# Four copied half products in place of two scans that read their input from PSUM, in a two-layer state-space kernel

## The chip, the cores and the metric

One core of a Trainium2 chip runs one program that computes all 16 images. The metric is the time of one execution in device microseconds. Before the change the median of 3 runs is 21545.68 us (21533.71 to 21551.96).

## The reference, cut to what matters

Each image has 192 channels and 56x56 = 3136 positions. Layer 1 (an RWKV layer with a scan in both directions) is not touched. Layer 2 is a Mamba layer with 384 inner channels and 16 states for each, run once forward and once backward over the positions:

```
def step(h, inp):
    x_t, dt_t, B_t, C_t = inp
    dA = jnp.exp(dt_t[:, :, None] * A)
    h = h * dA + (dt_t * x_t)[:, :, None] * B_t[:, None, :]
    y = jnp.einsum('bdn,bn->bd', h, C_t)
```

For each channel and state four things are wanted at each position: the decay `exp(dt*A)`, the B product `(dt*x)*B`, the running `h`, and `h*C` summed over the states. `dt*x` is called `du` in the kernel.

## The kernel before, in words

The 3136 positions are 7 chunks of 448, taken forward (i = 0 to 6) and then backward (i = 7 to 13). A chunk has three tiles of 128 channels (e). A chunk's tile is called a **block** here (index r). A block's 16 states are eight **pairs** (q counts them over everything, p = 0 to 7 within a block). A pair is 128 rows by two runs of 448 columns with one column between them that carries the state from the previous chunk. There are 16 images x 14 chunks x 3 tiles = 672 blocks and 5376 pairs.

For each pair:
- ScalarE writes the two decays (L1370), one value between the runs (`reset`, L1380), and afterwards saves the last state (`carry`, L1388).
- One of three engines makes the B product: GpSimd (L1434) for p = 0, 2, 4; VectorE (L1206) for p = 1, 3, 5, from a copy of `du` that TensorE put into PSUM bank 4, `DUBANK` (job `dp`, L1013); TensorE (L1099) for p = 6, 7.
- VectorE runs the scan (L1222). It reads decays and products and writes `hh`.
- GpSimd multiplies by C (L1442), and TensorE adds over the states into bank 5, for two pairs at a time (L1123).

GpSimd's and VectorE's products go to a ring `bb` in SBUF of NB = 3 places, and the decays of those pairs to two double banks in PSUM (`DECAY`, banks 0 and 1 or 2 and 3). With TensorE's pairs it is the other way round: TensorE can write only PSUM, so its product goes into the pair's decay banks, and ScalarE writes the decays of these pairs into `bb`. The scan then takes its two inputs exchanged. TensorE's product is 16 matmuls (one for each of 2 states, 4 parts of 112 positions and 2 halves of the rows) of `duT`, the transposed `du` (jobs `dT`, TensorE, L1022, and `dS`, ScalarE, L1323), with `bz`, a block-diagonal arrangement of B that comes by DMA. A seventeenth matmul of one column (L1093) puts the carried state between the runs. When GpSimd's or VectorE's pair next uses the banks, ScalarE clears that column first (L1367).

Each engine works through one list in the order of steps g = q. VectorE at step g does scan(g), then a product for the pair g + 2, then the side jobs that are due. ScalarE at step g does the decays and the reset of pair g + 1, the carry of pair g - 1 (it waits for that scan), then its side jobs. TensorE at step g makes the product of pair g + 1 if it is its own (it waits for scan g - 1, since the banks must be free), then the sums for pairs g - 3 and g - 2 if g is odd, then its side jobs. GpSimd at step g does the output of pair g - 1, a product for pair g + 2, side jobs.

The side jobs prepare later blocks and finish earlier ones. `side_schedule` gives each a due time in steps, written out by hand: convolution (`cv`, TensorE L1054; `c1` to `c4` on ScalarE; `xc` on VectorE L1180), projections (`x` L1040, `xp` L1061 with `p1` on ScalarE L1304, `t` L1066 with `t1` L1310, `z` L1071, `o` L1078), the step size (`td`, L1186) and `du` (L1423). `ye` takes the finished sums out of bank 5: on ScalarE in the forward half (L1328, due early in step 1 of the next block), on VectorE in the backward half (L1193, due in step 2). The first matmul of the next block into bank 5 (L1115) waits for it. Every engine takes its list strictly in order, so a wait holds up all that follows on that engine.

## Time and profile before

| | |
|---|---|
| median of 3 runs | 21545.68 us |
| profiled execution | 21543.77 us |
| its span | 21542.0 us |
| TensorE busy, share of the span | 84% |
| VectorE busy | 77% |
| GpSimd busy | 74% |
| ScalarE busy | 63% |
| mean granted TensorE clock | 0.892 |

The 16 images take 1346 us each and are alike. A busy share is an average over both layers. The profile's TensorE matmuls are recorded as two records each (float32), and their ends are modelled.

### The profile page before, as it was taken

The page shows a single profiled execution, that of the slowest core. Times are in us where ns is not written, and L with a number is a line of the kernel's source. Part 1 is how long each engine was busy: PE and PEld are TensorE (multiplying, and loading weights), DVE is VectorE, ACT ScalarE, POOL GpSimd, SP SyncE. Part 2 cuts the span into 40 slices and gives each one's busy share as a digit, 9 for nine tenths or more (in the row PEclk, how much of TensorE's full clock was granted, in tenths as well). Part 3 has the DMA queues.
Part 4 walks back from the last instruction along what each step waited for, and adds up shares of the span by engine and source line. Part 5 has one row for each costly group of instructions (what it writes and reads, how often), then busy time and mean ns, then how long its engine had stood idle before and what let it go on. Part 6 is the DMA issues. An engine that isn't in the chain of part 4 may idle for free. (4 is left out here: it accounts for less than half of the span.)

```text
span 21542.0 us, 288881 instructions
## 1 busy us (share of the span) xinstructions
PE 18146.0 (84%) x93536; PEld 8343.5 (39%) x93536; DVE 16650.5 (77%) x12912; ACT 13602.1 (63%) x35141; POOL 15848.3 (74%) x10356
## 2 busy tenths in 40 slices
PE   7888888888888888888888888888888888888888
PEld 3433434344343443434434344343443434434344
DVE  7877878778787787877878778787787877878778
ACT  5656656566565665656656566565665656656566
POOL 5867868678686786867868678686786867768677
PEclk8988989889898898988989889898998989989899
DMA  2424424234242442424424244242442424324243
GB/s 73 110 59 100 110 63 109 63 99 108 63 109 63 100 106 63 109 64 100 105 63 109 64 101 104 63 109 64 103 102 63 110 65 105 98 63 111 64 108 96
DMA packets 1351547, 1906.07 MB, mean 88 GB/s; under 512 B 588266, under 2 KB 1094340, under 8 KB 1349892
## 3 DMA queue, kind: packets, MB, share of 16 engines
q1 hardware_dynamic: 1349892, 1886.24, 35.4%
q8 instruction: 766, 12.55, 0.3%
q14 instruction: 889, 7.28, 0.1%
HBM read 1160.53 MB, written 248.04 MB: 65 GB/s over the span
## 5 line engine op out<-in xcount | busy, mean ns | idle before, releaser
L1442 POOL TENSOR_TENSOR arena<-arena 128x896 f32<-128x896 f32 x5376 | 9442.9, 1765 | 3148.9 <-DVE arena L1222 2512.2
L1222 DVE TENSOR_TENSOR_SCAN arena<-ps,arena 128x897 f32<-128x897 f32 x4032 | 8263.6, 2066 | 626.5 <-POOL arena L1434 296.0
L1370 ACT ACTIVATE ps<-arena,A 128x448 f32<-128x448 f32 x8064 | 4782.6, 626 | 1056.3 <-DVE arena L1222 940.1
L1123 PE MATMUL ps<-arena,rep 128*64 128x448 f32 x21504 | 5181.4, 609 | 101.3 <-POOL arena L1442 101.3
L1222 DVE TENSOR_TENSOR_SCAN arena<-arena,ps 128x897 f32<-128x897 f32 x1344 | 2782.7, 2070 | 2610.0 <-PE ps L1099 856.6
L1434 POOL TENSOR_TENSOR arena<-arena 128x896 f32<-128x896 f32 x2016 | 3567.6, 1770 | 622.2 <-DMA arena<-arena 609.9
L1123 PEld LDWEIGHTS ps<-arena,rep 128*64 128x64 f32 x21504 | 1480.1, 151 | 3050.3 <-issue 2449.9
L1099 PE MATMUL ps<-arena 112*64 112x112 f32 x43008 | 2592.5, 278 | 0.0
L1099 PEld LDWEIGHTS ps<-arena 112*64 112x64 f32 x43008 | 2276.5, 147 | 20.2
L1054 PE MATMUL ps<-arena,diag 128*128 128x448 f32 x5248 | 2149.4, 553 | 111.8 <-ACT arena L1323 74.7
L1206 DVE TENSOR_TENSOR arena<-ps,arena 128x896 f32<-128x896 f32 x2016 | 2148.7, 1066 | 121.8 <-DMA arena<-bc_rows 121.8
L1370 ACT ACTIVATE arena<-arena,A 128x448 f32<-128x448 f32 x2688 | 1635.8, 658 | 0.0
L1115 PE MATMUL ps<-arena,skipd 128*128 128x448 f32 x1344 | 840.3, 713 | 901.3 <-DVE arena L1193 760.1
L1054 PEld LDWEIGHTS ps<-arena,diag 128*128 128x128 f32 x5248 | 968.3, 191 | 1223.4 <-issue 1039.7
L1066 PE MATMUL ps<-arena,wdt 13*128 13x448 f32 x1344 | 816.8, 717 | 508.0 <-DVE arena L1186 496.5
L1388 ACT ACTIVATE arena<-arena 128x2 f32<-128x2 f32 x5376 | 1034.8, 192 | 222.3 <-DVE arena L1222 221.7
L1323 ACT ACTIVATE arena<-ps 112x512 f32<-112x512 f32 x672 | 398.4, 593 | 1181.3 <-PE ps L1022 1181.2
L1423 POOL TENSOR_TENSOR arena<-arena 128x448 f32<-128x448 f32 x672 | 654.2, 978 | 512.8 <-DVE arena L1186 512.8
L1093 PE MATMUL ps<-arena,ident 128*128 128x1 f32 x2304 | 438.0, 259 | 663.7 <-DVE arena L1222 637.4
L1093 PEld LDWEIGHTS ps<-arena,ident 128*128 128x128 f32 x2304 | 408.7, 209 | 1421.3 <-DVE arena L1222 860.1
L868 POOL TENSOR_TENSOR arena<-arena 128x448 f32<-128x448 f32 x336 | 347.4, 1034 | 711.9 <-DVE arena L614 711.9
L1367 ACT ACTIVATE ps<-zero 128x1 f32<-128x1 f32 x1312 | 222.2, 169 | 980.8 <-DVE arena L1222 980.8
(184 smaller groups left out, 24756.2 us busy)
## 6 DMA issues: line engine op xcount, KB each, us to landing
arena<-bc_rows SPq DMA_DIRECT2D x3136, 224.0 KB, 4.9
arena<-arena SPq DMA_DIRECT2D x4160, 112.0 KB, 3.0
arena<-b_diagonals SPq DMA_DIRECT2D x224, 784.0 KB, 7.0
x_projected<-arena SPq DMA_DIRECT2D x112, 672.0 KB, 3.6
y_forward<-arena SPq DMA_DIRECT2D x112, 672.0 KB, 5.5
arena<-x_projected SPq DMA_DIRECT2D x112, 672.0 KB, 4.8
arena<-y_forward SPq DMA_DIRECT2D x112, 672.0 KB, 4.8
x<-in_x SPq DMA_DIRECT2D x119, 336.0 KB, 3.6
```

Source lines behind the costliest of these rows:

```text
L1054: m = e.matmul(o, diag[:, k, q, :], xh[i % 2][:, k, h:h + T], start=q == 0, stop=q == 3)
L1066: e.matmul(o, wdt[s][:, k * 128:(k + 1) * 128], res[0:R + 1, :], start=True, stop=True).then_inc(c_wt, 1)
L1093: e.matmul(ps[:, b, RS:RS + 1], ident[:, :], car[:, 2 * k + h, n:n + 1] if i % NC else zero[:, 0, 0:1], start=True, stop=True)
L1099: m = e.matmul(ps[64 * j:64 * j + 64, b + a, o:o + TB], duT[:, r % NDR, n, 64 * h:64 * h + 64], bz[:, n, (2 * j + a) * TB:(2 * j + a + 1) ...
L1115: e.matmul(y, skipd[:, s, k, :], xc[:, r % NXC, :], start=True, stop=False)
L1123: m = e.matmul(ps[64 * h:64 * h + 64, YBANK, 0:T], rep[:, 0:64], pr[:, (q - 1 + h) % NPR, a * T:a * T + T], start=False, stop=p == NP - 1 ...
L1206: e.tensor_tensor(two(bb[:, q % NB, :]), ps[:, DUBANK, 0:T].unsqueeze(1).to_broadcast([128, 2, T]), br[:, p - 1:p + 1, :], ALU.mult).then_ ...
L1222: e.tensor_tensor_scan(rev(hh[:, q % NH, 0:W2], s), rev(f, s), rev(b, s), car[:, 2 * k + p % 2, n:n + 1] if i % NC else 0.0, ALU.mult, ALU ...
L1370: e.activation(o[:, a, :], dt2[:, r % NR2, p % 2, :], ACT.Exp, scale=Am[s][:, 2 * k + p % 2, n:n + 1]).then_inc(c_ex, 1)
L1388: e.activation(car[:, 2 * k + p % 2, n:n + 2], h[:, 0:T1 + 1:T1] if s else h[:, T - 1:W2:T1], ACT.Copy).then_inc(c_ca, 1)
L1434: e.tensor_tensor(two(bb[:, q % NB, :]), du2[:, r % NR2, :].unsqueeze(1).to_broadcast([128, 2, T]), br[:, p:p + 2, :], ALU.mult).then_inc( ...
L1442: e.tensor_tensor(pr[:, q % NPR, :].rearrange("p (a b) -> p a b", a=2), two(hh[:, q % NH, :]), cr[:, p - p % 2:p - p % 2 + 2, :], ALU.mult ...
```

## The change

- TensorE's products no longer go to the decay banks. Each becomes two runs of 8 matmuls, one for each state (`sb`, four runs m = 0 to 3 in a block), written to columns 0 to 447 of `DUBANK`, one after another. After each run ScalarE copies the bank to the ring `bb` (`se`, 128x448). The runs are side jobs at steps 3.1, 4.1, 5.1 and 6.1 of their block, the copies at 3.6, 4.6, 5.6 and 6.3.
- A run waits for the copy of the run before, the first one for VectorE's last product of the block. `dp` waits for the block's last copy, and is due at the earliest one step later than before.
- The scan reads decays from PSUM and products from `bb` for every pair. The matmul of one column (L1093), ScalarE's clearing (L1367) and their waits go. `reset` puts the carried state in for all pairs.
- The ring `bb` has 4 places instead of 3.
- VectorE's products for p = 1, 3, 5 are made after scans 0, 1, 2 of the block (`LEAD`), where they were made after scan 7 of the block before, and scans 1 and 3.

```diff
-RS = 511
+LEAD = {1: 1, 3: 2, 5: 3}
-NB, NH, NPR = 3, 3, 4
+NB, NH, NPR = 4, 3, 4
...
-        pe.append((max(NP * (EJ * i + e) - 2, t + 4.5), "dp", i, e))
+        pe.append((max(NP * (EJ * i + e) - 1, t + 4.5), "dp", i, e))
...
+        for m in range(4):
+            o = NP * (EJ * i + e) + 3 + m
+            pe.append((o + 0.1, "sb", i, 4 * e + m))
+            act.append((o + (0.6 if m < 3 else 0.3), "se", i, 4 * e + m))
...
         else:
-            w.wait_ge(c_be, NE[q + 1])
+            w.wait_ge(c_ev, 2 * NE[q + 1])
...
                     w.wait_ge(c_bv, NV[NP * r])
+                    w.wait_ge(c_ev, 4 * r)
...
+                if name == "sb":
+                    k, m = divmod(k, 4)
+                    r = EJ * i + k
+                    h, a = divmod(m, 2)
+                    w.wait_ge(s_zl, 16 * (i + 1))
+                    freed(w, "dT", i, k)
+                    w.wait_ge(c_bv, NV[NP * (r + 1)])
+                    w.wait_ge(c_ev, 4 * r + m)
+                    for n in range(NTB):
+                        for j in range(2):
+                            m = e.matmul(ps[64 * j:64 * j + 64, DUBANK, TB * n:TB * n + TB],
+                                         duT[:, r % NDR, n, 64 * h:64 * h + 64],
+                                         bz[:, n, (2 * j + a) * TB:(2 * j + a + 1) * TB], start=True, stop=True)
+                    m.then_inc(c_be, 1)
...
-            if 0 <= g + 1 < Q and maker(g + 1) == PE:
-                product(g + 1)
...
-            if g + AHEAD < Q and maker(g + AHEAD) == DVE:
-                product(g + AHEAD)
+            for n in LEAD.values():
+                if 0 <= g + n < Q and maker(g + n) == DVE and LEAD[(g + n) % NP] == n:
+                    product(g + n)
...
+                if name == "se":
+                    k, m = divmod(k, 4)
+                    r = EJ * i + k
+                    q = NP * r + 6 + m // 2
+                    w.wait_ge(c_be, 4 * r + m + 1)
+                    w.wait_ge(c_sc, q - NB + 1)
+                    o = m % 2 * T1
+                    e.activation(bb[:, q % NB, o:o + T], ps[:, DUBANK, 0:T], ACT.Copy).then_inc(c_ev, 1)
...
-            if maker(q) == PE:
-                w.wait_ge(c_sc, q - NB + 1)
-                o = two(bb[:, q % NB, :])
-            else:
-                w.wait_ge(c_sc, q - 1)
-                o = two(decays(q))
-                if q > 1 and maker(q - 2) == PE:
-                    e.activation(ps[:, DECAY[q % 2], RS:RS + 1], zero[:, 0, 0:1], ACT.Copy).then_inc(c_rz, 1)
+            w.wait_ge(c_sc, q - 1)
```

## Rows read from the trace of the kernel before

**Rows 1.** The page's busy time, share and instructions by engine.

```profile
PE 18146.0 (84%) x93536; PEld 8343.5 (39%) x93536; DVE 16650.5 (77%) x12912; ACT 13602.1 (63%) x35141; POOL 15848.3 (74%) x10356
```

**Rows 2.** Busy time by stretch, layer 2, forward and backward half of one image.

```profile
core 0: us, PE busy (x) PEld busy (x) DVE busy (x) ACT busy (x) POOL busy (x), PEclk, DMA share, GB/s
4400.00:4850.00 450.00, 383.17 (x2185) 184.52 (x2185) 356.81 (x236) 298.54 (x804) 360.48 (x220) 0.90 0.40 101
4850.00:5395.00 545.00, 477.16 (x2704) 223.35 (x2702) 446.02 (x311) 362.51 (x978) 441.87 (x273) 0.92 0.42 105
```

**Rows 3.** Groups by line: count | busy, mean ns | idle before, releasers.

```profile
L1222 DVE TENSOR_TENSOR_SCAN arena<-ps,arena 128x897 f32<-128x897 f32 x4032 | 8263.6, 2066 | 626.5 <-POOL arena L1434 296.0 <-ACT arena L1388 208.8 <-ACT ps L1370 54.2
L1222 DVE TENSOR_TENSOR_SCAN arena<-arena,ps 128x897 f32<-128x897 f32 x1344 | 2782.7, 2070 | 2610.0 <-PE ps L1099 856.6 <-ACT arena L1388 697.2 <-ACT ps L1370 509.9
L1206 DVE TENSOR_TENSOR arena<-ps,arena 128x896 f32<-128x896 f32 x2016 | 2148.7, 1066 | 121.8 <-DMA arena<-bc_rows 121.8
L1093 PE MATMUL ps<-arena,ident 128*128 128x1 f32 x2304 | 438.0, 259 | 663.7 <-DVE arena L1222 637.4 <-issue 26.3
L1093 PE MATMUL ps<-zero,ident 128*128 128x1 f32 x384 | 70.5, 253 | 41.6 <-DVE arena L1222 40.9
L1099 PE MATMUL ps<-arena 112*64 112x112 f32 x43008 | 2592.5, 278 | 0.0
L1115 PE MATMUL ps<-arena,skipd 128*128 128x448 f32 x1344 | 840.3, 713 | 901.3 <-DVE arena L1193 760.1 <-ACT arena L1328 141.2
L1370 ACT ACTIVATE ps<-arena,A 128x448 f32<-128x448 f32 x8064 | 4782.6, 626 | 1056.3 <-DVE arena L1222 940.1 <-DMA arena<-arena 104.2
L1370 ACT ACTIVATE arena<-arena,A 128x448 f32<-128x448 f32 x2688 | 1635.8, 658 | 0.0
L1328 ACT ACTIVATE arena<-ps 128x448 f32<-128x448 f32 x336 | 178.6, 532 | 373.7 <-PE ps L1123 373.7
L1367 ACT ACTIVATE ps<-zero 128x1 f32<-128x1 f32 x1312 | 222.2, 169 | 980.8 <-DVE arena L1222 980.8
L1323 ACT ACTIVATE arena<-ps 112x512 f32<-112x512 f32 x672 | 398.4, 593 | 1181.3 <-PE ps L1022 1181.2
L1304 ACT ACTIVATE arena<-ps,ident 64x448 f32<-64x448 f32 x224 | 140.7, 628 | 999.3 <-PE ps L1061 999.3
```

**Rows 4.** Timeline, a backward block's last steps: start, us, engine, line [idle before <-releaser].

```profile
5026.77 3.27 PE L1054 MATMUL ps<-arena,diag 128*128 128x448 f32 x8
5029.88 0.28 PE L1093 MATMUL ps<-arena,ident 128*128 128x1 f32 x2
5030.09 1.54 PEld L1099 LDWEIGHTS ps<-arena 112*64 112x64 f32 x32
5030.09 1.75 PE L1099 MATMUL ps<-arena 112*64 112x112 f32 x32
5031.95 2.08 DVE L1222 TENSOR_TENSOR_SCAN arena<-arena,ps 128x897 f32<-128x897 f32 x1 [1.81 <-PE ps L1099]
```

**Rows 5.** Timeline, ScalarE over one step of the same block.

```profile
5024.64 1.20 ACT L1370 ACTIVATE ps<-arena,A 128x448 f32<-128x448 f32 x2
5025.77 0.19 ACT L1380 ACTIVATE arena<-arena 128x1 f32<-128x1 f32 x1
5025.86 0.19 ACT L1388 ACTIVATE arena<-arena 128x2 f32<-128x2 f32 x1
5025.95 0.62 ACT L1335 ACTIVATE arena<-ps,bxz 128x448 f32<-128x448 f32 x1
```

**Rows 6.** Timeline, TensorE after two long waits, backward and forward.

```profile
5075.19 1.46 PE L1115 MATMUL ps<-arena,skipd 128*128 128x448 f32 x2 [4.86 <-DVE arena L1193]
5078.36 3.25 PE L1123 MATMUL ps<-arena,rep 128*64 128x448 f32 x8
5083.82 1.67 PE L1123 MATMUL ps<-arena,rep 128*64 128x448 f32 x8
...
4513.03 0.59 PE L1093 MATMUL ps<-arena,ident 128*128 128x1 f32 x2 [4.78 <-DVE arena L1222]
4513.55 3.25 PE L1099 MATMUL ps<-arena 112*64 112x112 f32 x32
```

**Rows 7.** Busy time by stretch around those waits; the granted clock is the seventh number.

```profile
5075.00:5082.00 7.00, 6.81 (x14) 2.02 (x14) 6.70 (x5) 4.04 (x12) 4.92 (x5) 0.54 0.86 208
4513.00:4517.00 4.00, 3.97 (x36) 3.78 (x38) 2.62 (x3) 1.68 (x7) 3.74 (x3) 0.50 0.00 0
```

**Rows 8.** Timeline, TensorE before a product of a forward block.

```profile
4484.11 1.77 PE L1040 MATMUL ps<-arena,wx 96*128 96x448 f32 x4
4485.72 3.17 PE L1054 MATMUL ps<-arena,diag 128*128 128x448 f32 x8
4488.93 1.75 PE L1099 MATMUL ps<-arena 112*64 112x112 f32 x32
```

More of the change, by code:

```diff
@@ L167, in side_schedule @@
     release = {(name, i, e): read.get((last.get(name), i, e)) for _, name, i, e in plans[0]}
-    for k, (t, name, i, e) in enumerate(a for a in plans[0] if a[1] != "dp"):
+    for k, (t, name, i, e) in enumerate(a for a in plans[0] if a[1] not in ("dp", "sb")):
         banks = WBANK if t >= -10 else [*WBANK, 0, 1, 2, 3]
@@ L1082, in side @@
                     busy(e, *behind.get((name, k), (0, 0)))
-        def product(q):
-            r, i, k, p, s = pair(q)
-            b, h = DECAY[q % 2], p % 2
-            w.wait_ge(s_zl, 16 * (i + 1))
-            freed(w, "dT", i, k)
-            w.wait_ge(c_sc, q - 1)
-            n = p - h + 1 - s
-            if i % NC:
-                w.wait_ge(c_ca, q - PER + 1)
-            e.matmul(ps[:, b, RS:RS + 1], ident[:, :], car[:, 2 * k + h, n:n + 1] if i % NC else zero[:, 0, 0:1],
-                     start=True, stop=True)
-            for a in range(2):
-                for n in range(NTB):
-                    for j in range(2):
-                        o = (RS - T) * (1 - a) + TB * n
-                        m = e.matmul(ps[64 * j:64 * j + 64, b + a, o:o + TB],
-                                     duT[:, r % NDR, n, 64 * h:64 * h + 64],
-                                     bz[:, n, (2 * j + a) * TB:(2 * j + a + 1) * TB], start=True, stop=True)
-            m.then_inc(c_be, 1)
         side(-10)
         for g in range(-2, Q + LAG):
-            if 0 <= g + 1 < Q and maker(g + 1) == PE:
-                product(g + 1)
             q = g - LAG
@@ L1137, in layer1_vector @@
         for b in DECAY:
-            e.memset(ps[:, b, RS:RS + 1], 0.0)
+            e.memset(ps[:, b, T:T1], 0.0)
         steps = Steps(plan_dve)
@@ L1216, in scan @@
             n = p - p % 2 + s
-            f, b = decays(q)[:, 0:W2], bb[:, q % NB, 0:W2]
-            if maker(q) == PE:
-                f, b = b, f
-            if maker(q - 2) == PE and maker(q) != PE and q > 1:
-                w.wait_ge(c_rz, NE[q - 1])
-            e.tensor_tensor_scan(rev(hh[:, q % NH, 0:W2], s), rev(f, s), rev(b, s),
+            e.tensor_tensor_scan(rev(hh[:, q % NH, 0:W2], s), rev(decays(q)[:, 0:W2], s), rev(bb[:, q % NB, 0:W2], s),
                                  car[:, 2 * k + p % 2, n:n + 1] if i % NC else 0.0, ALU.mult, ALU.add).then_inc(c_sc, 1)
@@ L1359, in decay @@
                     w.wait_ge(c_wf[b], first.get(b, 0))
[L1360 to L1367 removed]
+            w.wait_ge(c_sc, q - 1)
             for a in range(2):
                 n = p - p % 2 + a
[L1370 removed]
+                e.activation(two(decays(q))[:, a, :], dt2[:, r % NR2, p % 2, :], ACT.Exp,
                              scale=Am[s][:, 2 * k + p % 2, n:n + 1]).then_inc(c_ex, 1)
@@ L1376, in reset @@
             w.wait_ge(c_sc, q - NB + 1)
-            given = i % NC and maker(q) != PE
-            if given:
+            if i % NC:
                 w.wait_ge(c_ca, q - PER + 1)
-            e.activation(bb[:, q % NB, T:T1], car[:, 2 * k + p % 2, n:n + 1] if given else zero[:, 0, 0:1],
+            e.activation(bb[:, q % NB, T:T1], car[:, 2 * k + p % 2, n:n + 1] if i % NC else zero[:, 0, 0:1],
                          ACT.Copy).then_inc(c_rs, 1)
```

14 lines of the change are left out of this document (6 added, 8 removed).

## The prediction

> **What bounds the kernel now.** I read the page's busy times first. TensorE is busiest with 84%, VectorE 77%, GpSimd 74%, ScalarE 63% [rows 1]. No engine is full, so the waits decide. Only layer 2 changes, so next come the stretches inside layer 2: TensorE 383 of 450 us forward and 477 of 545 backward (85 and 88%), VectorE 79 and 82%, GpSimd 80 and 81%, ScalarE 66 and 67% [rows 2]. Then the groups by line, for the idle time before each. VectorE's scans of GpSimd's and its own products waited 626.5 us in 4032 scans. The scans that take TensorE's product waited 2610.0 us in 1344, which is 1.94 us each and 12% of the span [rows 3]. Only 856.6 us of that ended with TensorE's product. 697.2 and 509.9 us ended with ScalarE's carry and decays, and ScalarE in turn waits for TensorE: 1181.3 us before the copy of the transposed `du`, 999.3 us before the projection's copy [rows 3]. TensorE waits for VectorE: 663.7 + 41.6 us before the one-column matmul and 760.1 us before L1115, for `ye` [rows 3]. So the bound is a circle of three in-order queues, and TensorE, with the least idle time, is the one that is late. A row of it: a convolution of 3.27 us stands ahead of the product, the product starts 2 us late, and the scan waits 1.81 us [rows 4].
>
> **The change, part by part.** All sums are over the 672 blocks, against the profiled execution's 21543.8 us. The median shown is 1.9 us above that, so it needs no scaling.
>
> (a) The one-column matmul and its wait for scan g - 1 go. Busy 438.0 + 70.5 us, idle before it 663.7 + 41.6 us, together 1213.8 us of TensorE's queue, 1.81 us a block [rows 3]. Since TensorE is the late queue, I count this whole as the gain. If it were not late, the wait would only turn up at its next instruction. The ends are 0 and 1214.
>
> (b) Two products become four runs. The matmuls stay the same. A product takes 1.75 us (2592.5 / 1344 = 1.93 us on average [rows 3]) while its weight loads take 1.54 [rows 4], so each start costs about 0.21 us of filling. Two more starts a block are 672 x 0.42 = 282 us. The ends are 0 (the next work follows in the pipe) and 282. I take 282, because a run's end is now what ScalarE waits for.
>
> (c) A run waits for the copy of the run before. No row of before has this copy, but `ye` on ScalarE is the same shape from PSUM to SBUF: 532 ns [rows 3]. Runs 0 and 2 are followed by TensorE's next step with no sums in between for runs 1 and 3, so two waits a block can show: 672 x 2 x 0.53 = 712 us. In the backward list a side job stands in between in three of six places (the convolution due at 3.5, `xp` at 13.1, `dT` and `z` at 21.1 and 21.6), and hides the copy. I take half, 356 us. The ends are 0 and 712.
>
> (d) VectorE's products move to after scans 0, 1 and 2. In the backward half `ye` is due in step 2 and now has the product for p = 5 ahead of it, 1066 ns [rows 3]. L1115 waits for `ye`, and behind L1115 in TensorE's queue are the sums and run 0. 336 backward blocks x 1.066 = 358 us. If also the product moved into step 0 counts, it is 716. If TensorE is late anyway, it is 0. I take 358, since TensorE does wait here today. In the forward half ScalarE's `ye` is in step 1, and I put this at nothing.
>
> (e) ScalarE gets four copies a block and loses the clearing (222.2 us in all) and 32 ns on each of 2688 decays that now go to PSUM (658 against 626 ns) [rows 3]: 2688 x 0.532 - 222 - 86 = 1122 us more work. A step's fixed work takes 1.31 us, from the start of the decays to the start of the side job [rows 5]. With a copy it is 1.84, under a scan's 2.07. ScalarE is idle a third of layer 2, so I take 0. That cover is gone wherever the copy comes late (the second rival). The upper end is 1122.
>
> (f) The fourth place costs nothing and brings little. GpSimd's product for g + 2 stands behind the output of g - 1, which waits for the same scan that frees a place of three. It lets the copies for p = 6 start one scan earlier. DMA issues are the same in number and bytes. `bl`, which waits for products, comes free no later. `dp` is due one step later and waits for the last copy; it has until the end of the next block's scan 0, some 4 us for its 1 us. I take 0, up to 100 if it is late in a block of three.
>
> Sum: 1214 - 282 - 356 - 358 = 218 us less, 0.32 us a block. 21543.8 - 218 + 1.9 = 21328, say **21,330 us**, 1.0% faster. What is late next is the same circle: the convolution still stands ahead of run 1 or run 3, and a scan still waits for it.
>
> **Rivals.** *Much faster: the circle opens.* The products leave the banks that the scans alternate in, and no longer need to be made within one scan's time. If the waits that ended with TensorE's product go and nothing takes their place, it is 21545 - 857 = 20,690 us. If half of the other 1753 us goes too, it is 19,810. For it speaks that the run 0 could be made early. Against it: the due times put all four runs and copies into steps 3 to 6, right before the scans that need them, and and the idle time before all scans, 626.5 + 2610.0 us [rows 3], is only 4.8 us a block to begin with.
>
> *Slower: late copies hold ScalarE, and ScalarE holds every scan.* Before, TensorE's lateness reached ScalarE only at the side jobs. Now ScalarE stops at four places a block, in steps 3 to 6, behind TensorE's queue, and the decays of two pairs on stand behind each copy. ScalarE can be some 0.7 us late (2.07 - 1.31) before a scan waits [rows 5]. In the first forward block of a chunk `x` and the convolution, 1.77 + 3.17 us [rows 8], stand between run 0 and run 1. With the run's own 0.9 us that is 5.8 us in a step that gives 2.07 and a slack of 0.7: a scan would wait 3.0 us, against the 1.94 us that a scan with TensorE's product waits today on average, so 112 x 1.1 = 120 us. In the backward half `ye` is later, TensorE sits idle at L1115 for longer, and afterwards it is slow: after an idle of 4.86 us the granted clock is 0.54, near the lower of the two levels, and sums take 3.25 us instead of 1.67; after 4.78 us of idle a product takes 3.25 instead of 1.75 at a clock of 0.50 [rows 6, 7]. The sums lose 1.6 us, and L1115 takes 1.46 us against 840.3 / 672 = 1.25 on average [rows 3], together 1.8 us. In the backward chunk that I read, one block of three has such a wait today. In the other two it would come new: 224 x 1.8 = 400 us, all of it ahead of run 0. 21,545 - 218 + 120 + 400 = 21,850 us. It decides from 0.32 us a block of scans held up by late copies.
>
> The Trainium skill, "TensorE: Matmul & The Clock Gate", section on HAM oscillation, says that a loop which waits between bursts of matmuls falls back to the low clock and starts each burst slow. The trace agrees in the rows of that rival. By the rule without the trace the new waits of the backward half would each start the next burst at half speed, which is this rival's time and not the forecast's.
>
> *No change.* The 1.81 us that (a) frees is met by as much waiting for copies: (b), (c) and (d) at their upper ends are 282 + 712 + 716 = 1710, at their lower ones 0, and 1214 lies inside. That is 21,545 us.
>
> **How the numbers follow.** I give the forecast 0.33, the much faster case 0.24, no change 0.10, slower 0.33. A change of 0.2% (43 us) is about what a measurement of this kernel can tell from none. So faster by more has 0.57, within it 0.10, slower 0.33. The forecast's own range is 21,000 to 21,500. The whole range reaches into both rivals, 20,500 to 22,000 us: below it lies the part of the much faster case in which ScalarE's waits go as well (0.08), above it a slower case in which copies hold up more than two blocks in three (0.10).
>
> **What would show it.** (a) TensorE's busy share in the stretches of layer 2 rises above 85 and 88%, and none of its product's matmuls waits for a scan. (b, c) Each run is 16 records and starts within 0.2 us of its copy's end where no side job stands between. (d) L1115's idle time behind the backward `ye` grows from 760 by about 360 us. (e) The new copies take 0.53 us. If they show large idle times before them, above 1.5 us each, and the scans for p = 5 and 6 wait for ScalarE's decays, the slower rival is right. If the waits before the scans for p = 6 and 7 fall from 2610 to below 1700 us with none new elsewhere, the much faster one is. The granted clock falls below 0.89 in the slower case and rises in the others. I am wrong if scans at p = 4 and 5, which wait little today, take over the waiting.

## The result and the profile after

The changed kernel takes 22606.12 us, the median of 4 runs (22592.56 to 22633.41). The kernel before takes 21539.69 us beside it (21522.74 to 21551.96, 4 runs). The ratio is 1.0497 with an interval of 1.0479 to 1.0515, so it is 1066 us slower. I had forecast 21,330 us, within 20,500 to 22,000. Both are missed. Of the rivals the one on the slower side came nearest (21,850 us).

The page's busy times of the changed kernel, against [rows 1]:

```profile
PE 18112.9 (80%) x90848; PEld 8004.3 (35%) x90848; DVE 16684.3 (74%) x12912; ACT 14585.3 (65%) x36517; POOL 15864.4 (70%) x10356
```

Its stretches of one image, forward and backward half, against [rows 2], and seven microseconds after a long wait of TensorE, against [rows 7]:

```profile
core 0: us, PE busy (x) PEld busy (x) DVE busy (x) ACT busy (x) POOL busy (x), PEclk, DMA share, GB/s
4600.00:5050.00 450.00, 372.56 (x2114) 169.89 (x2111) 353.85 (x233) 321.86 (x832) 350.93 (x214) 0.91 0.40 100
5095.00:5655.00 560.00, 446.40 (x2430) 202.40 (x2426) 412.23 (x287) 358.88 (x933) 404.29 (x249) 0.88 0.36 91
5210.00:5217.00 7.00, 6.36 (x45) 3.33 (x46) 0.88 (x1) 2.42 (x7) 3.60 (x3) 0.66 0.93 224
```

TensorE's share is 83% forward and 80% backward. It had been 85 and 88%, and I had said it would rise. The busy times of the engines are within 35 us of those before, apart from ScalarE's, which is 983 us longer. So time went into waiting, and the backward half shows most of it. From the first to the last of one image's 21 `ye` that half takes 568.4 us in place of 508.9. The forward half takes 523.2 in place of 518.8. Times 16 images these are 952 and 70 us, together 1022 of the 1049 us between the two profiled spans.

The groups by line of the changed kernel. The scan is L1215, VectorE's product L1204, `dp` L1018, `xc` L1178, `td` L1184, `ye` L1191 (backward) and L1330 (forward). The first matmuls of a block into bank 5, which wait for `ye`, are L1113; they are called the **skip products** here. The sums are L1121, the runs L1031, the copies L1320, decays and carry L1365 and L1382, and VectorE's part of the output is L1196:

```profile
L1215 DVE TENSOR_TENSOR_SCAN arena<-ps,arena 128x897 f32<-128x897 f32 x5376 | 10998.2, 2067 | 3294.6 <-ACT arena L1382 1881.0 <-ACT arena L1320 826.5 <-POOL arena L1428 463.1
L1204 DVE TENSOR_TENSOR arena<-ps,arena 128x896 f32<-128x896 f32 x2016 | 2161.0, 1072 | 528.3 <-PE ps L1018 528.3
L1178 DVE SCALAR_TENSOR_TENSOR arena<-ps,vece,arena 128x448 f32<-128x448 f32 x672 | 451.9, 672 | 502.8 <-ACT arena L1290 502.8
L1184 DVE SCALAR_TENSOR_TENSOR arena<-ps,arena 128x448 f32<-128x448 f32 x672 | 405.5, 614 | 423.3 <-ACT arena L1312 423.3
L1196 DVE SCALAR_TENSOR_TENSOR x<-ps,bout,x 96x448 f32<-96x448 f32 x224 | 151.0, 674 | 239.7 <-PE ps L1098 239.7
L1320 ACT ACTIVATE arena<-ps 128x448 f32<-128x448 f32 x2688 | 1446.7, 538 | 3091.0 <-PE ps L1031 3089.4
L1031 PE MATMUL ps<-arena 112*64 112x112 f32 x43008 | 2798.7, 271 | 574.0 <-ACT arena L1320 552.9 <-DVE arena L1204 14.6
L1113 PE MATMUL ps<-arena,skipd 128*128 128x448 f32 x1344 | 932.0, 785 | 1234.9 <-DVE arena L1191 1127.7 <-ACT arena L1330 105.8
L1121 PE MATMUL ps<-arena,rep 128*64 128x448 f32 x21504 | 5289.8, 618 | 392.2 <-POOL arena L1436 378.2
```

Four rows of the kernel before, for comparison: `xc`, `td` and the output job of VectorE (L1178, L1184, L1196 after the change) and TensorE's sums (L1121 after).

```profile
L1180 DVE SCALAR_TENSOR_TENSOR arena<-ps,vece,arena 128x448 f32<-128x448 f32 x672 | 448.2, 667 | 300.3 <-ACT arena L1296 300.3
L1186 DVE SCALAR_TENSOR_TENSOR arena<-ps,arena 128x448 f32<-128x448 f32 x672 | 405.1, 613 | 190.9 <-ACT arena L1318 190.9
L1198 DVE SCALAR_TENSOR_TENSOR x<-ps,bout,x 96x448 f32<-96x448 f32 x224 | 151.4, 676 | 59.9 <-PE ps L1078 59.9
L1123 PE MATMUL ps<-arena,rep 128*64 128x448 f32 x21504 | 5181.4, 609 | 101.3 <-POOL arena L1442 101.3
```

Read this as two accounts of idle time. **VectorE** is idle 1015 us more (22590.7 - 16684.3 against 21542.0 - 16650.5). The scans have only 58 of it, 3294.6 in place of 626.5 + 2610.0 [rows 3]. The other waits grew: the products for `dp` by 406, `xc` by 203, `td` by 232, L1196 by 180. But the scans wait for something else. TensorE's product ended 856.6 us of their waits before, and ScalarE's carry some 906 in the two groups together [rows 3]. Now the carry ends 1881.0 us and the copies 826.5. **TensorE** is idle 1082 us more, though the 705 us before the one-column matmul are gone. The waits that came are 574 before the runs, 334 before the skip products (1234.9 against 901.3), and 291 before the sums. Its busy time fell by 33 us only, though 508 us of one-column matmuls went: the runs took 206 more, the sums 108, the skip products 92.

The timeline of one backward block of the changed kernel (start, us, engine, line, and in brackets the idle time before and its releaser), against [rows 6]:

```profile
5206.29 0.61 DVE L1191 TENSOR_TENSOR arena<-arena,ps 128x448 f32<-128x448 f32 x1
5206.96 1.86 PE L1113 MATMUL ps<-arena,skipd 128*128 128x448 f32 x2 [5.55 <-DVE arena L1191]
5208.75 1.86 PE L1086 MATMUL ps<-arena,wdt 13*128 13x448 f32 x2
5210.54 3.26 PE L1121 MATMUL ps<-arena,rep 128*64 128x448 f32 x8
5210.64 0.55 ACT L1304 ACTIVATE arena<-ps 128x448 f32<-128x448 f32 x1 [4.33 <-PE ps L1086]
5213.58 1.50 PE L1031 MATMUL ps<-arena 112*64 112x112 f32 x16
5215.13 0.54 ACT L1320 ACTIVATE arena<-ps 128x448 f32<-128x448 f32 x1 [3.94 <-PE ps L1031]
5215.57 1.19 ACT L1365 ACTIVATE ps<-arena,A 128x448 f32<-128x448 f32 x2
5215.73 0.99 PE L1031 MATMUL ps<-arena 112*64 112x112 f32 x16 [0.65 <-ACT arena L1320]
5216.54 1.68 PE L1121 MATMUL ps<-arena,rep 128*64 128x448 f32 x8
5217.06 2.08 DVE L1215 TENSOR_TENSOR_SCAN arena<-ps,arena 128x897 f32<-128x897 f32 x1 [6.19 <-ACT arena L1382]
...
5237.82 1.86 PE L1113 MATMUL ps<-arena,skipd 128*128 128x448 f32 x2 [4.67 <-DVE arena L1191]
5242.35 1.72 PE L1121 MATMUL ps<-arena,rep 128*64 128x448 f32 x8
5244.89 0.55 ACT L1320 ACTIVATE arena<-ps 128x448 f32<-128x448 f32 x1 [7.18 <-PE ps L1031]
5246.82 2.08 DVE L1215 TENSOR_TENSOR_SCAN arena<-ps,arena 128x897 f32<-128x897 f32 x1 [4.49 <-ACT arena L1382]
```

TensorE stands idle for 5.55 us until `ye` is done. Then it is slow: the sums take 3.26 us and not 1.68. So run 0 ends more than 8 us after `ye` began. ScalarE has first waited 4.33 us for the projection `t` (L1086), which stands behind the skip products as well. Then it has reached copy 0 and waits 3.94 us for run 0. The decays of p = 5 stand behind this copy, though they need nothing from it, and the scan of p = 5 starts 6.19 us late.

The slow sums of this block are not new. The kernel before had 4.86 us of idle time and sums of 3.25 us in its block of the same kind [rows 6]. Its scan of p = 5 there waited 0.30 us:

```profile
5080.40 2.08 DVE L1222 TENSOR_TENSOR_SCAN arena<-ps,arena 128x897 f32<-128x897 f32 x1 [0.30 <-ACT arena L1388]
```

What is new here is that ScalarE waits for run 0, so that TensorE's lateness reaches the decays.

The three blocks of a backward chunk differ. From one `ye` to the next the changed kernel takes 30.9, 33.2 and 24.7 us (starts 5206.29, 5237.16, 5270.37, 5295.05), where the kernel before takes 25.9, 26.3 and 26.2 us in blocks of the same kinds. In the second block the skip products wait 4.67 us and are slow (1.86 us for the pair), but the sums run at full speed (1.72 us). Copy 0 waits 7.18 us, and the scan of p = 5 waits 4.49. In the third the skip products wait for nothing, and the block is 1.5 us shorter than before. So two blocks of three lose, and the slow clock came new in one of them.

### The profile page after: what moved, and what is told of

The parts are those of the page before. It is cut to its first block and busy times, and to the rows that moved or that the text cites. A ratio compares the mean times of both kernels' runs of the same rounds, so it can differ in the third digit from the quotient of the medians.

```text
span 22590.7 us, 281969 instructions
## 1 busy us (share of the span) xinstructions
PE 18112.9 (80%) x90848; PEld 8004.3 (35%) x90848; DVE 16684.3 (74%) x12912; ACT 14585.3 (65%) x36517; POOL 15864.4 (70%) x10356
## 5 line engine op out<-in xcount | busy, mean ns | idle before, releaser
L1215 DVE TENSOR_TENSOR_SCAN arena<-ps,arena 128x897 f32<-128x897 f32 x5376 | 10998.2, 2067 | 3294.6 <-ACT arena L1382 1881.0
L1365 ACT ACTIVATE ps<-arena,A 128x448 f32<-128x448 f32 x10752 | 6399.8, 631 | 1671.1 <-DVE arena L1215 1536.7
L1121 PE MATMUL ps<-arena,rep 128*64 128x448 f32 x21504 | 5289.8, 618 | 392.2 <-POOL arena L1436 378.2
L1320 ACT ACTIVATE arena<-ps 128x448 f32<-128x448 f32 x2688 | 1446.7, 538 | 3091.0 <-PE ps L1031 3089.4
L1031 PE MATMUL ps<-arena 112*64 112x112 f32 x43008 | 2798.7, 271 | 574.0 <-ACT arena L1320 552.9
L1031 PEld LDWEIGHTS ps<-arena 112*64 112x64 f32 x43008 | 2372.3, 144 | 1850.5 <-issue 924.8
L1121 PEld LDWEIGHTS ps<-arena,rep 128*64 128x64 f32 x21504 | 1463.8, 150 | 3369.1 <-issue 2240.4
L1204 DVE TENSOR_TENSOR arena<-ps,arena 128x896 f32<-128x896 f32 x2016 | 2161.0, 1072 | 528.3 <-PE ps L1018 528.3
L1113 PE MATMUL ps<-arena,skipd 128*128 128x448 f32 x1344 | 932.0, 785 | 1234.9 <-DVE arena L1191 1127.7
L1086 PE MATMUL ps<-arena,wdt 13*128 13x448 f32 x1344 | 775.2, 684 | 560.6 <-DVE arena L1184 473.8
L1382 ACT ACTIVATE arena<-arena 128x2 f32<-128x2 f32 x5376 | 1040.5, 194 | 33.9 <-DVE arena L1215 33.9
L1374 ACT ACTIVATE arena<-arena 128x1 f32<-128x1 f32 x4608 | 883.3, 192 | 0.0
L1113 PEld LDWEIGHTS ps<-arena,skipd 128*128 128x128 f32 x1344 | 275.1, 244 | 1675.1 <-DVE arena L1191 1297.7
L1098 PE MATMUL ps<-arena,wout 128*96 128x448 f32 x1344 | 690.9, 665 | 167.5 <-ACT arena L1354 167.5
L1178 DVE SCALAR_TENSOR_TENSOR arena<-ps,vece,arena 128x448 f32<-128x448 f32 x672 | 451.9, 672 | 502.8 <-ACT arena L1290 502.8
L1091 PE MATMUL ps<-arena,wz 96*128 96x448 f32 x1344 | 708.0, 659 | 57.3 <-ACT arena L1325 37.4
```

The source lines that it names most:

```text
L1031: m = e.matmul(ps[64 * j:64 * j + 64, DUBANK, TB * n:TB * n + TB], duT[:, r % NDR, n, 64 * h:64 * h + 64], bz[:, n, (2 * j + a) * TB:(2 * ...
L1113: e.matmul(y, skipd[:, s, k, :], xc[:, r % NXC, :], start=True, stop=False)
L1121: m = e.matmul(ps[64 * h:64 * h + 64, YBANK, 0:T], rep[:, 0:64], pr[:, (q - 1 + h) % NPR, a * T:a * T + T], start=False, stop=p == NP - 1 ...
L1204: e.tensor_tensor(two(bb[:, q % NB, :]), ps[:, DUBANK, 0:T].unsqueeze(1).to_broadcast([128, 2, T]), br[:, p - 1:p + 1, :], ALU.mult).then_ ...
L1215: e.tensor_tensor_scan(rev(hh[:, q % NH, 0:W2], s), rev(decays(q)[:, 0:W2], s), rev(bb[:, q % NB, 0:W2], s), car[:, 2 * k + p % 2, n:n + 1 ...
L1320: e.activation(bb[:, q % NB, o:o + T], ps[:, DUBANK, 0:T], ACT.Copy).then_inc(c_ev, 1)
```

## The experiments

Times are medians. The kernel before took 21,540 to 21,555 us beside each.

### Where `ye` stands

*ye in step 1* (the changed kernel):

```
-                dve.append((t + 1.5, "ye", i, e))
+                dve.append((t + 0.5, "ye", i, e))
```

> The changed kernel with one number different: the backward half's ye on VectorE is due in step 1 of the next block (t + 0.5) and not in step 2, so that it stands ahead of scan 2 and of the product for p = 5. Theory A (the loss comes from ye behind VectorE's three early products: TensorE idles at L1113, is slow afterwards, run 0 is late, ScalarE waits for it): the backward half gets most of its 57 us an image back, 22,606 goes to 21,700 to 21,900, L1113's idle time falls from 1235 us to below 600. Theory B (the copies themselves are due too close behind their runs, whatever ye does): less than 300 us come back, 22,300 or more.

Measured: 21635.36 us, ratio 1.0037 [1.0021, 1.0053]. One due time gives back 971 of the 1066 us.

```profile
L1215 DVE TENSOR_TENSOR_SCAN arena<-ps,arena 128x897 f32<-128x897 f32 x5376 | 10982.3, 2067 | 2368.0 <-ACT arena L1320 947.6 <-ACT arena L1382 840.0 <-POOL arena L1428 457.1
L1113 PE MATMUL ps<-arena,skipd 128*128 128x448 f32 x1344 | 749.1, 642 | 397.4 <-DVE arena L1191 286.4 <-ACT arena L1330 109.6
```

The scans lose 927 us of idle time; what ended with the carry falls by 1041, what ended with copies grows by 121. The skip products and sums behind one `ye`:

```profile
5114.10 1.02 PE L1113 MATMUL ps<-arena,skipd 128*128 128x448 f32 x2 [1.69 <-DVE arena L1191]
5116.69 1.72 PE L1121 MATMUL ps<-arena,rep 128*64 128x448 f32 x8
5118.24 0.94 PE L1031 MATMUL ps<-arena 112*64 112x112 f32 x16
5119.23 0.55 ACT L1320 ACTIVATE arena<-ps 128x448 f32<-128x448 f32 x1 [1.73 <-PE ps L1031]
```

This is a block of the second kind. The skip products wait 1.69 us in place of 4.67 and take 1.02 us in place of 1.86. Run 0 ends 5.7 us after `ye` began, and copy 0 waits 1.73 us in place of 7.18. Two blocks of the first kind, where `t` stands between skip products and sums:

```profile
5087.29 1.02 PE L1113 MATMUL ps<-arena,skipd 128*128 128x448 f32 x2 [1.57 <-DVE arena L1191]
5089.34 3.21 PE L1121 MATMUL ps<-arena,rep 128*64 128x448 f32 x8
...
5167.95 1.02 PE L1113 MATMUL ps<-arena,skipd 128*128 128x448 f32 x2 [0.74 <-DVE arena L1191]
5169.84 1.72 PE L1121 MATMUL ps<-arena,rep 128*64 128x448 f32 x8
```

In this image two early chunks of the half still have slow sums there, behind idle times of 1.81 and 1.57 us; the chunks after them have 0.74 us and sums at full speed. Three blocks take 78 to 80 us, as before the change. TensorE's granted clock rises from 0.886 to 0.912, and its busy time falls by 435 us for the same instructions (17678.0 in place of 18112.9).

*ye in step 2, ahead of the product for p = 5.* This is the 1.07 us that my term (d) charged:

```
-                if 0 <= g + n < Q and maker(g + n) == DVE and LEAD[(g + n) % NP] == n:
+                if n < 3 and 0 <= g + n < Q and maker(g + n) == DVE and LEAD[(g + n) % NP] == n:
...
+            if g + 3 < Q and (g + 3) % NP == 5:
+                product(g + 3)
```

> The changed kernel with ye still in step 2 (after scan 2, with that step's other side jobs), but VectorE's product for p = 5 put behind the side jobs instead of ahead of them. It takes away only the 1.07 us of that product from ye; ye in step 1 took away the product and scan 2, 3.1 us, and gave 971 us. If the prediction's term (d) is the whole of it: about 336 x 1.07 = 360 us come back, 22,250. If it is a threshold (TensorE's idle time before L1113 just long enough for the low clock): 600 us or more. If ye's place behind scan 2 is what counts: less than 150.

Measured: 22606.9 us, ratio 1.0496 [1.0475, 1.0517], as the changed kernel. Two groups, and TensorE's timeline behind one `ye`:

```profile
L1113 PE MATMUL ps<-arena,skipd 128*128 128x448 f32 x1344 | 861.1, 730 | 894.2 <-DVE arena L1191 779.5 <-ACT arena L1332 113.3
L1121 PE MATMUL ps<-arena,rep 128*64 128x448 f32 x21504 | 5519.8, 641 | 393.5 <-POOL arena L1438 378.8
```

```profile
5221.11 1.86 PE L1113 MATMUL ps<-arena,skipd 128*128 128x448 f32 x2 [3.01 <-DVE arena L1191]
5224.69 3.11 PE L1121 MATMUL ps<-arena,rep 128*64 128x448 f32 x8
```

The wait at the skip products shrank by 341 us, which is just 336 x 1.01. But 3.01 us of idle are followed by nearly the same slow sums (3.11 us) as 5.55 us were. TensorE's busy time is 380 us longer (18492.5) at a clock of 0.869, and its idle time is 360 us shorter (22610.0 - 18492.5 = 4117.5 against 4477.8). What the shorter waits gave went into slower matmuls. So (d) had the size of the idle time right, and taking this idle time away by itself gives nothing back.

*ye in step 1 in the kernel before:*

```
-                dve.append((t + 1.5, "ye", i, e))
+                dve.append((t + 0.5, "ye", i, e))
```

> The kernel before with ye in step 1 alone. VectorE's product for p = 5 is not in step 2 there (it is in step 3), so ye moves only past one scan, and may wait for TensorE's sums. Theory A: a small gain or none, 21,350 to 21,600, since L1115's idle time of 901 us is partly ye's. If it gains as much as the changed kernel did (971 us), the change was not what made ye's place expensive, and theory A is wrong.

Measured: 21873.39 us, ratio 1.0153 [1.0124, 1.0182]. There the same edit costs 332 us. The wait at the skip products halves as well, and `ye` now waits for the sums (339.3 us; 116.7 before it was moved):

```profile
L1115 PE MATMUL ps<-arena,skipd 128*128 128x448 f32 x1344 | 785.1, 670 | 424.7 <-DVE arena L1193 282.9 <-ACT arena L1328 141.8
L1193 DVE TENSOR_TENSOR arena<-arena,ps 128x448 f32<-128x448 f32 x336 | 207.2, 617 | 339.3 <-PE ps L1123 339.3
```

### The places of VectorE's products

*The kernel before with the change's places for the products, and nothing else:*

```
+LEAD = {1: 1, 3: 2, 5: 3}
...
-            if g + AHEAD < Q and maker(g + AHEAD) == DVE:
-                product(g + AHEAD)
+            for n in LEAD.values():
+                if 0 <= g + n < Q and maker(g + n) == DVE and LEAD[(g + n) % NP] == n:
+                    product(g + n)
```

> The kernel before with VectorE's products made after scans 0, 1 and 2 (the LEAD edit alone; no runs, no copies, three places). Theory A in its plain form says that ye comes a product later here too and TensorE idles at L1115 longer: 21,540 goes up by 300 to 500 us. Theory C (ye is only harmful together with copies that ScalarE takes in order): within 150 us of 21,540, L1115's idle time up by 300 us all the same. Theory B says no change.

Measured: 22081.77 us, ratio 1.0254 [1.0224, 1.0284], 530 us slower. So a loss half as large comes without any run or copy.

```profile
L1223 DVE TENSOR_TENSOR_SCAN arena<-arena,ps 128x897 f32<-128x897 f32 x1344 | 2784.8, 2072 | 2883.7 <-PE ps L1100 1337.4 <-ACT arena L1390 776.7 <-ACT arena L1382 306.2
L1116 PE MATMUL ps<-arena,skipd 128*128 128x448 f32 x1344 | 887.2, 750 | 1287.3 <-DVE arena L1194 1152.6 <-ACT arena L1330 134.7
```

*Only p = 5 moved* (`{1: 2, 3: 2, 5: 3}`):

> The kernel before with VectorE's product for p = 5 alone moved, from after scan 3 to after scan 2. All three moves together cost 530 us, and ye in step 1 did not give them back. Theory D: VectorE's products fill time in which TensorE and ScalarE catch up; taken out of steps 3 to 7 they leave five scans in a row, and the wait before pairs 6 and 7 grows by what they covered. The product for p = 5 leaves step 3, just before TensorE's pairs: I expect 150 to 350 us. In the backward half it also puts ye 1.07 us later.

Measured: 21684.82 us, 1.0057 [1.0034, 1.008], 130 us.

*Only p = 1 moved* (`{1: 1, 3: 2, 5: 2}`):

> The kernel before with the product for p = 1 alone moved, from after scan 7 of the block before to after scan 0. Theory D: it leaves step 7 and enters step 0; TensorE's pair 7 has just been scanned, the next pairs are GpSimd's and VectorE's, and little waits there: 50 to 250 us. The two moves add up to about 530 if each only takes its own cover away; if they sum to much less, it is the row of five scans that costs, and only both together make it.

Measured: 21809.95 us, 1.0119 [1.0089, 1.0148], 255 us. This product stands ahead of `ye` in VectorE's list before and after the move, and the move still costs twice what that of p = 5 does. I had put it at nothing. The two make 385 of the 530 us.

*Both, the products' places and `ye` in step 1, in the kernel before:*

> The kernel before with both VectorE edits: products after scans 0, 1, 2, and ye in step 1. No runs, no copies. Theory A: the 530 us that the early products cost alone come back, 21,450 to 21,650; what then lies between this and the changed kernel with ye in step 1 (21,635) is the price of runs and copies. The rival (the early products hurt by their place before the scans, not by ye): 21,900 or more.

Measured: 22032.07 us, 1.0227 [1.0197, 1.0256]. The wait at the skip products falls from 1287.3 to 449.9 us, and the time by 50. In this kernel, too, that wait is not what the products' places cost.

These kernels make a table on which the change's parts can be read:

| us | ye in step 2 | ye in step 1 |
|---|---|---|
| before | 21,545 | 21,873 |
| + products' places | 22,082 | 22,032 |
| + runs, copies, fourth place (the change) | 22,606 | 21,635 |

The runs and copies cost 524 us in the one column and gain 397 in the other. They have no price of their own.

### The copies

Two kernels shrink the copies or the runs; each leaves out part of the computation, as its expectation says.

*Thin runs*, from the changed kernel:

```
-                    for n in range(NTB):
+                    for n in range(1):
```

> The changed kernel with each run of TensorE cut from 8 matmuls to 2 (three quarters of the B products of pairs 6 and 7 are left out), all waits and copies kept. If TensorE's own work is what is late (the convolution and the sums ahead of a run, and the run): about 0.6 us less for each of four runs a block, 1600 us of TensorE's queue, and the time falls by 600 us or more. Theory A: the waits stay where they are, since they are for VectorE's ye and for the copy, and the time falls by less than 400 us.

Measured: 22070.61 us (one run).

*Short copies:*

```
-                    e.activation(bb[:, q % NB, o:o + T], ps[:, DUBANK, 0:T], ACT.Copy).then_inc(c_ev, 1)
+                    e.activation(bb[:, q % NB, o:o + 16], ps[:, DUBANK, 0:16], ACT.Copy).then_inc(c_ev, 1)
```

> The changed kernel with each of ScalarE's copies cut from 448 columns to 16 (the rest of the B products of pairs 6 and 7 stays out of the ring), all waits kept. Takes away some 0.36 us of each copy, 970 us of ScalarE's work. If ScalarE's added work were the cost, 600 us or more come back. Theories A and B both say that ScalarE is held by waiting, not by work: less than 350 us come back, and the 3091 us of idle time before the copies stay above 2500.

Measured: 22235.31 us (one run). The group of its copies:

```profile
L1320 ACT ACTIVATE arena<-ps 128x16 f32<-128x16 f32 x2688 | 479.4, 178 | 3481.4 <-PE ps L1031 3477.8
```

967 us of ScalarE's work bring 371 us, and the wait before the copies grows by 390. With a quarter of the matmuls in the runs, 536 us come back, between the two outcomes that were expected. TensorE's mean granted clock falls to 0.854 there, and the sums take 5553.4 us in place of 5289.8, so a part of what the thin runs save is lost again. Nor is it a price of the change, since the same matmuls were there before it. With either, the kernel is still 2.4 to 3.2% slower than before. So neither length by itself makes up the 1066 us; what is left lies in the waits and in the moved products.

*Copies on VectorE, ye in step 1*, to see what ScalarE's place in the chain costs:

```
-            act.append((o + (0.6 if m < 3 else 0.3), "se", i, 4 * e + m))
+            dve.append((o + 0.9, "se", i, 4 * e + m))
```

> The changed kernel with ye in step 1 and the four copies on VectorE, at the end of the steps in which they were on ScalarE. ScalarE then has no wait for a run and no work of 1450 us; VectorE gets 4 x 0.55 us a block, 1480 us, on its own scans' queue. If what costs is ScalarE's decays held by late runs: the decays are never late, but VectorE itself stops for each run; I expect 21,900 to 22,600, slower than 21,635, because VectorE has less to spare. A time below 21,600 would say that the copies' place on ScalarE was the fault.

Measured: 21582.03 us, 1.0026 [1.0014, 1.0037].

```profile
L1224 DVE TENSOR_TENSOR_SCAN arena<-ps,arena 128x897 f32<-128x897 f32 x5376 | 11074.8, 2068 | 541.9 <-POOL arena L1429 389.8 <-issue 26.2 <-ACT ps L1366 16.5
L1155 DVE COPY arena<-ps 128x448 f32<-128x448 f32 x2688 | 1638.8, 610 | 1243.5 <-PE ps L1031 1242.7
```

With no copy in ScalarE's list the scans hardly wait for ScalarE: 541.9 us of idle time in place of 2368.0 with `ye` in step 1, which is 1826 less. This fits waits at the carry that came through the copies. It does not prove it, because VectorE now stops ahead of its own copies and gives ScalarE time. VectorE pays 1638.8 us of copying and 1243.5 of waiting for the runs, together 2882. I had expected 21,900 us or more. The median lies 53 us under that of the version with ScalarE's copies, but the ranges overlap (21550.76 to 21641.79 against 21613.14 to 21639.58). By my own mark (below 21,600) the copies' place on ScalarE was at fault, but 53 us with overlapping ranges are too little to rest that on. Other waits of VectorE shrink as well, `dp` from 531.3 to 183.2 us.

### Other places for runs, copies and side jobs

*Runs ahead of the sums* (`o - 0.05` in place of `o + 0.1`, with ye in step 1):

> The changed kernel with ye in step 1 and each run due just before its step (2.95, 3.95, 4.95, 5.95), so that TensorE makes runs 0 and 2 before the sums of steps 3 and 5. If copies wait for runs because 1.5 us of sums stand ahead of runs 0 and 2: the idle time before the copies falls from 2140 us to below 1500 and the time below 21,400. If TensorE is then only made to wait for the copy before or for VectorE's product instead: within 100 us of 21,635, or slower.

Measured: 21965.03 us, 1.0196 [1.0166, 1.0225]. The scans wait 2894.2 us in all, against 2368.0. The rival of the expectation came true: TensorE waits 509.0 us for VectorE's product before the runs, where it waited 23.2, and 1191.1 before the runs in all, where it was 613.5. The wait of `ye` for the sums did not grow (313.0 us against 325.0).

*Backward convolutions and input projection moved out of steps 3 to 6* (with ye in step 1):

```
-            for e, v in enumerate((1.3, 6.0, 10.7)):
+            for e, v in enumerate((1.3, 8.7, 11.0)):
...
-            project(i, t + 15.6, (1.9, 2.3, 5.2), 1.5)
+            project(i, t + 16.7, (1.0, 1.4, 4.3), 0.9)
```

> The changed kernel with ye in step 1, and in the backward half the two TensorE jobs that stood between a block's runs put behind its last run: the convolution due at 3.5 goes to 6.2 (the next from 8.2 to 8.5), the projection xp with what hangs on it from 13.1 to 14.2. If the copies wait because a job of 2.2 to 3.3 us stands between two runs: the 2140 us of idle time before the copies fall below 1600 in the backward half's share, and the time below 21,450. If the wait only moves to what these jobs feed (c1, p1, the step size, GpSimd's du): within 100 us of 21,635.

Measured: 22825.45 us, 1.059 [1.0559, 1.062].

*The same with the copies on VectorE:*

> The same with the copies on VectorE. Measured with the old places: 21,582 against 21,635 with the copies on ScalarE. If the places of the jobs matter for whoever waits for the runs, this gains as much as the previous kernel does, to 21,400 or below, and beats the kernel before; if VectorE is now full (84% busy), less than 50 us.

Measured: 22926.52 us, 1.0637 [1.0606, 1.0667], 101 us more than with the copies on ScalarE.

*Convolutions alone moved* (`(2.0, 8.7, 11.0)`, so that the first has another place too):

> The changed kernel with ye in step 1 and only the backward convolutions moved: from 22.8, 3.5 and 8.2 to 23.5, 6.2 and 8.5; xp and what follows stay. The version with xp moved too was 1190 us slower than without. If that came from xp (its chain to du, GpSimd's product and the DMA is late): this one is within 200 us of 21,635, and below it if a job between runs 0 and 1 costs. If it came from the convolutions: 22,500 or more.

Measured: 22117.99 us, 1.0269 [1.0249, 1.029]. All three miss. In the first VectorE waits 737.0 us for `dp`, against 531.3 without the move, the scans 2853.4 against 2368.0, and `ye` 684.1 against 325.0, nearly all of it for the sums. With the convolutions alone `ye` waits 574.2 us. What within these moves costs so much was not taken apart further.

*The p = 1 product back after scan 7* (`{1: 2, 3: 2, 5: 3}`, with ye in step 1):

> The changed kernel with ye in step 1 and the product for p = 1 back after scan 7 of the block before, as before the change (p = 3 and p = 5 stay after scans 1 and 2). In the kernel before, moving p = 1 cost 255 us and p = 5 130 us. Theory D (the product covers a wait of the late steps) expects 100 to 255 us less than 21,635, a tie with the kernel before or a little better. The rival: the product for p = 1 needs du in PSUM bank 4, which TensorE can write only after the block's last copy, so VectorE now waits for it before scan 0 instead of after it: 21,650 to 22,000.

Measured: 22877.13 us, 1.062 [1.0603, 1.0638].

```profile
L1204 DVE TENSOR_TENSOR arena<-ps,arena 128x896 f32<-128x896 f32 x2016 | 2163.3, 1073 | 1777.4 <-PE ps L1018 1654.3 <-DMA arena<-bc_rows 122.0
```

`dp` can't come before the last copy has left the bank, and a product that asks for it a step earlier waits 1654.3 us for it instead of 531.3. So the change needs its late p = 1, and pays for it.

*The same with copies on VectorE:*

> The same with the copies on VectorE (21,582 with the product for p = 1 after scan 0). As above: theory D 21,330 to 21,500, the rival 21,650 or more. Here the last copy is VectorE's own, at the end of step 6, so that bank 4 comes free a little later.

Measured: 22430.58 us, 1.041 [1.0393, 1.0428]. Both are slower than even their rival range from 21,650 to 22,000 us.

*Runs and copies spread, ye in step 2.* This takes copy 0 from its place half a step behind run 0:

```
-            pe.append((o + 0.1, "sb", i, 4 * e + m))
-            act.append((o + (0.6 if m < 3 else 0.3), "se", i, 4 * e + m))
+            pe.append((o + (0.1, 0.6, 0.4, 0.1)[m], "sb", i, 4 * e + m))
+            act.append((o + (1.2, 1.1, 0.9, 0.3)[m], "se", i, 4 * e + m))
```

> The changed kernel with the backward ye where the change has it (step 2), but the runs spread (steps 3.1, 4.6, 5.4, 6.1) and each copy one step or so behind its run (steps 4.2, 5.1, 5.9, 6.3), in place of runs at 3, 4, 5, 6 and copies half a step behind them. If the price is the tight chain ye, skip and sums, run 0, copy 0, decays of p=5 on ScalarE, then copy 0's idle time goes and much of the 1066 us comes back with ye still in step 2: 21,700 to 22,100 us, clock above 0.89. If the price is ye's place itself (TensorE's idle time at the skip products, then half clock, whoever waits for the copies), nothing comes back: 22,500 to 22,700 us. If the later copies reach the output step too late, 22,800 us or more.

Measured: 22925.91 us, 1.0641 [1.0611, 1.067].

*The same with ye in step 1:*

> The same spread runs and copies with the backward ye in step 1. If copy 0 and copy 1 still hold ScalarE in that kernel (947 us of the scans' idle time lay behind the copies in the changed kernel with ye in step 1), this gives 21,350 to 21,500 us and beats the kernel before. If the places of the sums and side jobs are what counts, the moved runs cost as in the other moved versions: 21,900 to 22,300 us. No effect: 21,600 to 21,700 us.

Measured: 22397.05 us, 1.0391 [1.037, 1.0413]. The scans of the two:

```profile
L1215 DVE TENSOR_TENSOR_SCAN arena<-ps,arena 128x897 f32<-128x897 f32 x5376 | 10981.1, 2066 | 3860.7 <-ACT arena L1320 3015.4 <-POOL arena L1428 431.2 <-ACT arena L1382 197.2
```

```profile
L1215 DVE TENSOR_TENSOR_SCAN arena<-ps,arena 128x897 f32<-128x897 f32 x5376 | 10972.4, 2066 | 3327.2 <-ACT arena L1320 2599.3 <-POOL arena L1428 431.3 <-POOL arena L1436 196.5
```

The decays came free of the copies: the carry ends 197.2 us of the first kernel's waits, in place of 1881.0. This is the strongest sign that the waits at the carry came through the copies. But the scans of p = 6 and 7 then wait for the copies themselves, 3015.4 us. Both hopes failed. Steps 3 to 6 are tight from both sides: an early copy holds the decays, a late one holds its own scan. `ye` in step 1 gives 529 us here, where it gave 971 with the change's own places.

No version that I tried is faster than the kernel before.

## Why the prediction was wrong, by its own steps

**(a), the step that failed.** I counted the one-column matmul and its wait, 1214 us, as gain, since TensorE was the late queue. The instruction and the wait did go. But the time freed did not become time saved: in the changed kernel TensorE waits at other places, for engines that had not become earlier. The new waits before runs and sums, 574 + 291 us, already outweigh the 705 us of old ones. I had written that the wait would turn up at the next instruction if TensorE were not late, and then gave that case no weight in the sum. With (a) at its lower end of 0 and the other terms as taken the sum gives 21,546 + 996 = 22,542 us, close to the 22,606 measured. This is luck: (d) has 358 of the 996, and the run that takes its 1.07 us away gains nothing.

**(b)** was about right: the runs have 206 us more busy time than the products (282 forecast), and a run takes 0.94 to 0.99 us where half a product took 0.875.

**(c)** was too small as a wait: 553 us of TensorE's waits before the runs end with a copy, against 356, within my ends of 0 and 712.

**(d)** named a wait that grew as forecast, by 368 us behind the backward `ye` (760.1 to 1127.7) against 358. But an idle time is not a cost. Moving `ye` ahead of the product took 341 us of the wait before the skip products away and gave nothing back. Moving it a whole step earlier gave 971 us. I had also put the product that moved into step 0 at nothing in the value that I took. In the kernel before it alone costs 255 us, and p = 5 130.

**(e)** I took as covered by ScalarE's idle third. The copies' own length is worth some 371 us, as the short copies show. Their waits are 3091.0 us, 1.15 each, with the decays queued behind. This is not idle time on top: ScalarE is idle 8005 us in all (22590.7 - 14585.3), where it was 7940 (21542.0 - 13602.1). The 980.8 us before the clearing went, and 1181.3 us before the copy of the transposed `du` became 84.9. The waits moved to a place ahead of the decays.

**(f)** I gave `dp` 4 us to spare and at most 100 us. VectorE's products wait 528.3 us for it, where 121.8 us had ended with a DMA [rows 3].

**The slower rival** had the mechanism: copies hold ScalarE, ScalarE holds the scans through decays and carry, TensorE idles at the skip products and is then slow. The spread copies show that the carry's waits came through the copies (1881.0 us became 197.2), and the timeline shows the chain whole in one block of three. One of its marks was off: the copies' idle time was 1.15 us on average and not above 1.5. The others held: in the blocks shown the scan of p = 5 waits for ScalarE, 6.19 and 4.49 us, and the mean granted clock fell from 0.892 to 0.886. That p = 5 takes over the waiting was also my sign of being wrong. Its size, 305 us, was under a third of the 1066: I priced the slow clock behind each `ye` (400) and late copies of the forward half (120), and took the forecast's gain of 218 off. That gain is (a)'s, and it is not in the measured time. I had the slow clock come new in two blocks of three; in the steady chunks it came new in one, and that one's sums are not slow. The trace shows 952 us in the backward half and 70 in the forward one. What I left out were `dp` (406 us at VectorE), its jobs `xc`, `td` and L1196 (615 us, behind ScalarE and TensorE) and the products' new places.

The Trainium skill says, in "TensorE: Matmul & The Clock Gate", section on HAM oscillation, that a loop with waits between its bursts starts each burst slow. The runs agree in part. After 5.55 us and after 3.01 us of idle the sums take 3.26 and 3.11 us, after 0.74 us of idle with `ye` in step 1 they take 1.72. But with `ye` in step 1 they also took 3.21 us after 1.57 us of idle, and in the changed kernel 1.72 us after 4.67, where the skip products ahead of them were the slow ones (1.86 us). The length of the one wait ahead of a burst did not settle its speed.

**What stays open.** The table of six kernels shows that `ye`, the products' places and the runs don't add up, and no run names one link by which `ye` becomes 971 us. Copy 0's early place stands in the chain of the timeline, but spreading runs and copies made things worse. No run was made in which TensorE's clock alone differs, so how much of the 971 us the 435 us of faster matmuls make is not shown either.

## What to carry to other kernels

When three in-order queues wait for each other, idle time removed from one is no gain until a run shows that nothing else holds it. Ask of each wait which instruction stands behind it that does not need it; here the decays of p = 5 stood behind a copy that they did not need. And try the schedule edits of a change (places, due times) by themselves before the change that needs them: here the products' places cost 530 us alone, and one due time was worth 971.

## What the runs showed of the hardware that I had not expected

- A shorter wait of TensorE can come with a lower granted clock and be worth nothing. With `ye` 1 us earlier TensorE's idle time fell by 360 us and its busy time rose by 380 for the same 90848 instructions, the mean clock going from 0.886 to 0.869.
- The other way round, the version with `ye` in step 1 ran the same instructions in 435 us less at a mean clock of 0.912. That is as much as 45% of the 977 us between the two spans; that the clock alone brings it is not shown.
- An ACTIVATE copy of 128x448 from PSUM to SBUF took 538 ns on ScalarE and 610 ns as a copy on VectorE. With 16 columns it took 178 ns on ScalarE, from which I estimate 0.83 ns a column above a base of about 165 ((538 - 178) / 432, and 178 - 13).
